# Transposing the heads' rows with VectorE and ScalarE in place of TensorE, in a four-layer graph attention kernel

## What is computed

```python
def layer0(h, adj):                         # h = relu(layernorm(x))
    Wh = einsum('nf,hfd->hnd', h, W_heads)  # 8 heads
    e  = leaky_relu(s1[:, :, None] + s2[:, None, :])
    e  = where(adj > 0, e, -9e15)
    hp = einsum('hnm,hmd->hnd', softmax(e), Wh)
    feat = transpose(elu(hp), (1, 0, 2)).reshape(2048, 8 * 128)
    return feat @ W_out + b_out
x = x + layer0(relu(layernorm(x)), adj)
x = x + gelu(attention_1(relu(layernorm(x))))
x = x + elu(attention_2(relu(layernorm(x))))
x = x + elu(attention_3(relu(layernorm(x))))
```

## Time and profile before

| | before |
|---|---|
| three runs | 810.85, 812.53, 816.41 us (median 812.53) |
| the profiled execution | span 812.6 us |
| TensorE passes | busy 786.3 us (97% of the span) |
| VectorE | busy 618.8 us (76%) |
| ScalarE | busy 236.2 us (29%) |
| mean granted TensorE clock | 0.989 |

### The profile page before, as it was taken

One profiled execution on the slowest core, in us unless ns is written; L12 is line 12 of the kernel. 1 busy time (PEld: TensorE's weight loads), 2 busy tenths in 40 slices (PEclk: granted clock), 3 DMA queues, 4 the chain that ended last, 5 costly groups with the idle time before them and its releaser, 6 DMA issues. The chain is left out here.

```text
span 812.6 us, 16635 instructions
## 1 busy us (share of the span) xinstructions
PE 786.3 (97%) x6786; PEld 767.1 (94%) x6786; DVE 618.8 (76%) x1069; ACT 236.2 (29%) x637; POOL 16.1 (2%) x34
## 2 busy tenths in 40 slices
PE   8999999999999999999999999999899989998995
PEld 8699999999999999999999999999699979987995
DVE  4595987787777967978778777795599569966994
ACT  2966221140231122112114023113430162135212
POOL 3000000000000000000000000000000000000000
PEclk8899999999999999999999999999999999999998
DMA  9686000000000000000000000000000000000000
GB/s 282 216 290 249 27 1 27 26 0 26 26 0 26 0 26 26 0 26 0 26 26 0 26 25 0 0 1 2 0 2 1 2 1 1 2 1 0 0 26 26
DMA packets 13709, 29.26 MB, mean 36 GB/s; under 512 B 1264, under 2 KB 7408, under 8 KB 13680
## 3 DMA queue, kind: packets, MB, share of 16 engines
q1 hardware_dynamic: 10992, 19.93, 7.4%
q0 software_dynamic: 2688, 8.92, 3.2%
HBM read 27.73 MB, written 1.11 MB: 35 GB/s over the span
## 5 line engine op out<-in xcount | busy, mean ns | idle before, releaser
L316 PE MATMUL acc<-V,probs 128*128 128x129 f32 x5632 | 641.4, 275 | 5.2 <-DVE probs L690 5.2
L316 PEld LDWEIGHTS acc<-V,probs 128*128 128x128 f32 x5632 | 635.1, 192 | 9.3 <-DVE probs L690 4.9
L690 DVE SCALAR_TENSOR_TENSOR probs<-rho,t_now,adjT 128x1024 f32<-128x1024 f32 x352 | 432.4, 1279 | 36.3 <-PE acc L316 29.9
L730 DVE TENSOR_TENSOR X<-X,side 128x512 f32<-128x512 f32 x32 | 22.0, 688 | 84.1 <-PE side L337 84.1
L509 ACT ACTIVATE fill<-mean_now,empty 128x128 f32<-128x128 f32 x160 | 48.9, 394 | 108.8 <-DVE den L703 108.8
L522 ACT ACTIVATE hpT<-side 128x512 f32<-128x512 f32 x32 | 17.4, 594 | 130.3 <-PE side L330 130.3
L516 ACT ACTIVATE rows<-rows 128x512 f32<-128x512 f32 x44 | 27.8, 631 | 94.3 <-DVE rows L712 69.5
L712 DVE SCALAR_TENSOR_TENSOR rows<-acc,den,fill 128x128 f32<-128x128 f32 x160 | 43.2, 342 | 4.5 <-ACT fill L509 4.1
L460 ACT ACTIVATE V<-side,v_now 128x128 f32<-128x128 f32 x128 | 36.1, 364 | 0.0
L261 PE MATMUL side<-W,hT 128*128 (+1 forms) x256 | 34.8, 280 | 0.0
L458 ACT ACTIVATE V<-v_now 128x4 f32<-128x4 f32 x32 | 6.7, 209 | 95.7 <-PE side L261 95.7
(11 more groups left out here) (105 smaller groups left out, 291.6 us busy)
## 6 DMA issues: line engine op xcount, KB each, us to landing
stage<-in_adj_t_dram SPq DMA_DIRECT2D x32, 512.0 KB, 7.1
rho<-rho_dram POOLq DMA_DIRECT2D x15, 512.0 KB, 3.8
X<-in_x_dram SPq DMA_DIRECT2D x2, 512.0 KB, 4.5
out_dram<-X SPq DMA_DIRECT2D x2, 512.0 KB, 3.2
W0t<-in_W_t_dram SPq DMA_DIRECT2D x1, 512.0 KB, 7.1
W<-in_L_gnn_W_heads_dram SPq DMA_DIRECT2D x1, 512.0 KB, 7.3
Wout<-in_L_gnn_W_out_dram POOLq DMA_DIRECT2D x1, 512.0 KB, 9.2
WL<-in_L_gnn_W_dram POOLq DMA_DIRECT2D x2, 64.0 KB, 5.4
```

What stands on the lines that cost most here:

```text
L316: last = nc.tensor.matmul(group(c, k), probs[:, j % RING, k * P:(k + 1) * P], V[:, j, :], start=(j == 0 and k % PER_BANK == 0), stop=(j == ...
L690: nc.vector.scalar_tensor_tensor(probs[:, j % RING, :], rho[:, c * CH:(c + 1) * CH], t_now[:, j:j + 1], adjT[:, j, c * CH:(c + 1) * CH], A ...
L730: nc.vector.tensor_tensor(at, at, side[:, b, :].rearrange("p (k d) -> p k d", k=4), ALU.add).then_inc(x_added, 1)
```

## The change

The transposes of the rows of units 0 to 14 are no longer done by TensorE. `elu` ends with one more VectorE instruction, a `transpose` of the whole 128 x 1024 tile from `rows[:, 0]` to `rows[:, 1]`, which turns every 32x32 block in its place. ScalarE's `move_blocks` then copies, in 16 instructions of 32 partitions x (8 x 32) elements each, the block column at partitions a and features b to partitions b and columns a of `hpT`. TensorE no longer takes part: `transpose_rows` and `T_AT` are gone, the waits that kept `side` free are now just ahead of `out_projection`, which stays behind tile 10 (`OUT_AT`). On VectorE `divide` goes from behind tile 9 to behind tile 8, and `elu` from behind tile 11 to behind tile 10. The last unit, u = 15, keeps TensorE's transposes (`transpose_last_rows`) and ScalarE's two copies.

```diff
--- before.py
+++ after.py
@@ -29,7 +29,8 @@
     PER_BANK = 512 // VW
     NB = -(-NK // PER_BANK)
     STAGE = 5
-    T_AT, DEN_AT = 8, 7
+    OUT_AT, DEN_AT = 10, 7
+    Q = 32
     PER_LATE = 36
 
     WARM = 20
@@ -321,14 +322,17 @@
                         if at == j:
                             work()
 
-            def transpose_rows(u, q):
+            def transpose_last_rows(u):
                 pe.wait_ge(elu_ready, u + 1)
-                pe.wait_ge(x_added, 2 * u + 1)
-                pe.wait_ge(v_ready, q * 4 + 4)
                 for b in range(2):
                     for k in range(4):
                         last = nc.tensor.transpose(side[:, b, k * P:(k + 1) * P], rows[:, 0, 4 * b + k, :], ident[:, :])
                     last.then_inc(hpT_psum, 1)
+
+            def side_free(u, q):
+
+                pe.wait_ge(x_added, 2 * u + 1)
+                pe.wait_ge(v_ready, q * 4 + 4)
 
             def out_projection(u, w):
                 for b in range(2):
@@ -339,7 +343,7 @@
                     last.then_inc(proj_psum, 1)
 
             def aside(u, q, w):
-                return ((T_AT, lambda: transpose_rows(u, q)), (T_AT + 2, lambda: out_projection(u, w)))
+                return ((OUT_AT, lambda: (side_free(u, q), out_projection(u, w))),)
 
             def head_of(t, h):
                 return t[:, bass.ds(h, 1), :].rearrange("p a d -> p (a d)")
@@ -395,7 +399,8 @@
             transpose_normed(1, 0)
             early_scores(1, wa1, WL[:, 0, :])
             pe.wait_ge(s1_copied, 2)
-            transpose_rows(2 * H - 1, H - 1)
+            side_free(2 * H - 1, H - 1)
+            transpose_last_rows(2 * H - 1)
             out_projection(2 * H - 1, Wout[:, H - 1, :])
             pe.wait_ge(wh_copied, 1)
             keep_warm(WARM_FIRST, idle)
@@ -516,9 +521,17 @@
                     nc.scalar.activation(rows[:, 1, 4 * b:4 * b + 4, :], rows[:, 0, 4 * b:4 * b + 4, :],
                                          func).then_inc(act_ready, 1)
 
+            def move_blocks(u):
+
+                act.wait_ge(elu_ready, u + 1)
+                for a in range(0, P, Q):
+                    for b in range(0, D, Q):
+                        last = nc.scalar.activation(hpT[b:b + Q, :, a:a + Q], rows[a:a + Q, 1, :, b:b + Q], ACT.Copy)
+                last.then_inc(hpT_ready, 2)
+
             def copy_transposed(u):
                 for b in range(2):
-                    act.wait_ge(hpT_psum, 2 * u + b + 1)
+                    act.wait_ge(hpT_psum, b + 1)
                     nc.scalar.activation(hpT[:, 4 * b:4 * b + 4, :], side[:, b, :].rearrange("p (k i) -> p k i", k=4),
                                          ACT.Copy).then_inc(hpT_ready, 1)
 
@@ -526,7 +539,7 @@
                 act.wait_ge(rden_ready, u + 1)
                 fill_rows(c)
                 nonlinear(u, ACT.Exp)
-                copy_transposed(u)
+                move_blocks(u)
 
             act.wait_ge(wa_psum, 1)
             nc.scalar.activation(wa0[:, :, :], score_bank[:, CW:CW + 2 * H].rearrange("p (h s) -> p s h", s=2),
@@ -716,12 +729,17 @@
                     if k % 4 == 3:
                         ins.then_inc(rows_ready, 1)
 
-            def elu(u):
+            def elu(u, transposed=True):
 
                 dve.wait_ge(act_ready, 2 * u + 2)
                 link(nc.vector.tensor_scalar(rows[:, 1, :, :], rows[:, 1, :, :], 1.0, 1.0, ALU.min, ALU.subtract))
-                nc.vector.scalar_tensor_tensor(rows[:, 0, :, :], rows[:, 0, :, :], 0.0, rows[:, 1, :, :],
-                                               ALU.max, ALU.add).then_inc(elu_ready, 1)
+                last = nc.vector.scalar_tensor_tensor(rows[:, 0, :, :], rows[:, 0, :, :], 0.0, rows[:, 1, :, :],
+                                                      ALU.max, ALU.add)
+                if transposed:
+                    link(last)
+                    last = nc.vector.transpose(rows[:, 1, :, :].rearrange("p k d -> p (k d)"),
+                                               rows[:, 0, :, :].rearrange("p k d -> p (k d)"))
+                last.then_inc(elu_ready, 1)
 
             def add_projection(u, c):
                 for b in range(2):
@@ -731,8 +749,8 @@
 
             def head0_asides(u, c, store=True):
                 return ((DEN_AT, lambda: denominators(u, c, store=store)),
-                        (DEN_AT + 2, lambda: divide(u, c, u)),
-                        (DEN_AT + 4, lambda: elu(u)),
+                        (DEN_AT + 1, lambda: divide(u, c, u)),
+                        (DEN_AT + 3, lambda: elu(u, store)),
                         (15, lambda: add_projection(u, c)))
 
             def add_elu(u, c):
@@ -784,7 +802,7 @@
                 dve.wait_ge(x_added, 1)
 
             unit(0, 0, rho_and_adj(0, 0, True), ((3, lambda: r_rows(0, 1, H)), (4, lambda: mean(0, 1)), (8, add_bias)))
-            PER = 1 + 2 * 3
+            PER = 1 + 2 * 4
             outside, steps[0] = steps[0], 0
             with dve.Fori(0, H - 1) as h:
                 base[0] = h * PER + outside
```

## The result

| | before | changed |
|---|---|---|
| median of 7 runs each | 814.03 us (810.85 to 816.41) | 809.04 us (806.98 to 810.80) |
| ratio | | 0.9931 (95% interval 0.9913 to 0.9949) |
| profiled execution, span | 812.6 us | 805.6 us |
| mean granted TensorE clock | 0.989 | 0.987 |

The kernel is faster by 0.7%, between 0.5 and 0.9%. The forecast was 802.0 us in a range of 799.0 to 806.0, and 1.3% faster. The sign is right, the size is half, and the time lies outside the range. An execution's time is 1.7 us (before) to 2.0 us (changed) above its span, and the later runs put the median of before at 814, not at 812.5. So the forecast span of 802.0 stands for a time of 804.0, and 3.6 us of the profiled span remain to be explained, 5.0 us of the median.

A forecast was written before the change was run, and what follows sets the result against it. TensorE was taken to bound the kernel: 13.2 us saved by removing its transposes, less a 2.6 us wait in unit 1, gives 10.6 us, so 812.6 - 10.6 = 802.0 us, range 799.0 to 806.0.

The forecast's parts named there:

- What bounds the kernel, and the removal: TensorE sets the pace from 85 to 560 us; dropping its transposes in units 0 to 14 saves 15 x 0.88 = 13.2 us.
- T: Time of the one added VectorE transpose per unit, taken as 1.23 us, bounds 0.69 and 2.29.
- The duration of a move: One ScalarE move of 256 columns on 32 partitions was taken to last 0.418 us.
- M: Time of a unit's 16 ScalarE moves together: overlapping, one every 0.31 us, 5.1 us, bounds 3.5 and 8.6.
- The chain of units 2 to 15: Transpose and moves fit before TensorE's output projection: in unit 7 they need 6.3 of 9.2 us, so no wait.
- Unit 1: ScalarE's late adjacency casts delay the fills and divisions, so TensorE waits 2.6 us for the moves at the output projection.
- rival 4: The wait in unit 1 lowers TensorE's clock, losing 3.2 us of work: 805.2 us; chance 0.07.
- The span set against the median: Profiled span and median of the runs differ by 0.1 us, so the forecast span stands for the median.
- The slower one: Moves do not overlap and take 0.631 us each, so TensorE waits in units 1 to 15: 832.6 us; chance 0.04.
- the sum: Waits summed over units 1 to 15 from T + M; the gain is gone at T + M = 10.0, M = 8.8 us.
- Rival 3: Nothing waits, not even unit 1: 799.4 us; chance 0.11 together with waits under 1.2 us.

The follow-up runs named there:

- b outer: The changed kernel with the same 16 moves reordered, so four in a row write the same partitions and read different ones; moves started 0.426 us apart.

## Why the prediction was wrong

**What bounds the kernel, and the removal: right.** TensorE's stream, and 13.2 us in it. The floor was reached twice, by leaving the moves out (13.0 us) and by taking the wait away (13.2).

**T: right**, 1.246 for 1.23. **The duration of a move: right**, 0.414 for 0.418.

**M: the term that was mis-sized.** "Consecutive ones overlap" was taken from the fills, which all work on the same 128 partitions. Each move reads or writes other partitions than the one before it, and such moves did not overlap: M = 6.8 and not 5.1, still inside the bounds of 3.5 and 8.6. It costs 1.7 us in unit 1 and none elsewhere.

**The chain of units 2 to 15: right** in that nothing waits. The spare time in unit 7 was 1.27 us; with the true M the prediction's 9.2 - 1.25 - 6.8 gives 1.15.

**Unit 1: the place and the cause right**, the wait 4.4 us for 2.6, of which M makes 1.7. The wait also differs from one execution to the next, since TensorE's arrival depends on the clock of the first 50 us and the moves' end on when the last pieces of the adjacency land: 4.4 and 3.55 us in two profiles of the same kernel, 5.28 in the form with b outer.

**The clock: the rival that should have been part of the forecast.** I gave it 0.07 and counted it as a case by itself. It came in the profiled execution, at 1.7 us, and not in the repeat; how many of the others have it is not known. The 3.2 us that rival 4 took, from the start of the kernel, were too much for this wait: where the idle stretch was 2.2 to 4.4 us the fall cost 1.5 to 1.7 us, and where it was 5.1 and 5.3 us, 2.9 and 3.0. The argument against it, gaps between 722 and 732 us with the clock kept, was about several short gaps. A gap in one piece is another matter. The profiles of the experiments show a fall behind idle stretches of 2.19, 2.85, 3.14, 3.44, 4.39, 5.08 and 5.28 us, and none behind 1.44, 3.52 and 3.55. The Trainium skill, "TensorE: Matmul & The Clock Gate", section "Why this matters for your kernels", warns of idle gaps between bursts of matmuls as what lowers the throughput; the traces agree in that the clock fell behind seven of these ten, and they add that the length alone does not decide.

**The span set against the median.** "The profiled span and the median of the runs differ by 0.1 us" was a coincidence of three runs, so this step of the forecast failed. The time of an execution is 1.7 to 2.0 us above its span, so the forecast should have read 804 us with the same differences. This alone accounts for 2.0 of the 7.0 us between 802.0 and 809.04; M for 1.7 and the clock for 1.7, as far as the profiled execution goes (its time is 807.67). The last 1.4 us are the distance from that execution to the median, whose span is 807.0 at a mean clock of 0.985, against 0.987; about 0.2 us are left over.

**The rivals.** The slower one, moves of 0.54 us and more, did not come. The sum had put the point where the gain is gone at M = 8.8; with twenty moves it is gone at 8.5, since the sum had no term for the clock. By the waits alone, 9.1 of 13.2 us, there would have been 4.1 us left. Rival 3, nothing waits, gave 799.4 and needs only the fills ahead of the last casts: 799.8 measured.

## What to carry to other kernels

When a step leaves the engine that bounds a kernel, look for the one iteration in which the helping engines are late for another reason (here the last casts ahead of unit 1): the steady loop had time to spare, and nearly half of the gain was lost in one unit. An idle stretch of a few microseconds on TensorE can cost more than its length, so a chain that just misses is worth a reordering; moving eight fills ahead of three casts gave back 6 us. Take the distance between starts of repeated instructions from rows whose neighbours share and change the same partitions as yours will, and set a sum of spans against spans.

## What the runs showed that was not expected

- ScalarE copies of 256 columns start 0.31 us apart where each reads and writes the same partitions as the one before it (32 or 128 of them), and 0.41 to 0.43 us apart where the next one reads or writes others. A move of 32 partitions costs no less than one of 128 (0.398 and 0.40 us).
- VectorE's 32x32 transposes of a float32 tile of 128 x 1024 take 1.246 us in one instruction, like a plain pass with two inputs (1.225 us).
- TensorE's clock, after idle stretches of nearly the same length in the same place, fell to the lower level in some executions (2.19 to 3.44 us, 4.39 us and more) and not in others (3.52, 3.55 us), the same kernel among them. What decides between them stays open: no run here tells it.
